# Output between the score halves, choice steps and one copy dealt anew, V read once a pass, projected rows' trips later

## The reference

```python
q = einsum('btc,hdc->bhtd', x, Wq); k = einsum('btc,hdc->bhtd', x, Wk)   # 16 heads of 64
w, sel = top_k(einsum('btc,hec->bthe', x, Ws), 2)                        # 2 of 8 experts per row and head
mix_v = einsum('bthk,bthke->bthe', sigmoid(w), one_hot(sel, 8))
v = einsum('bthe,bted->bhtd', mix_v, einsum('btc,edc->bted', x, Wv))
probs = softmax(einsum('bhid,bhjd->bhij', q * 64**-0.5, k), -1)
attn = einsum('bhij,bhjd->bihd', probs, v)
mask_o = one_hot(top_k(einsum('btc,hec->bthe', x, Wd), 2)[1], 8).sum(3)
res = einsum('bthe,bthd,efd->bthf', mask_o, attn, Wo).sum(2)
```

## Time and profile before

| | |
|---|---|
| median of 3 runs | 2452.25 us |
| the profiled execution | 2448.69 us |
| its span, first to last instruction | 2446.9 us |
| what lies around the span | 1.8 us |
| granted TensorE clock, mean | 0.993 |
| PE busy | 2341.4 us, 96% |
| ACT busy | 2079.9 us, 85% |
| DVE busy | 1964.1 us, 80% |
| POOL busy | 1138.2 us, 47% |

### The profile page before, as it was taken

The page is one execution under the profiler, slowest core; times in us unless marked ns, Lnnn a source line. Parts: engine busy times, 40 slices in busy tenths (PEclk is TensorE's granted clock), DMA queues, the critical chain, the costliest instruction groups (busy, mean ns, idle before and its releaser), DMA issues.

```text
span 2446.9 us, 120555 instructions
## 1 busy us (share of the span) xinstructions
PE 2341.4 (96%) x49920; PEld 2159.1 (88%) x49920; DVE 1964.1 (80%) x3498; ACT 2079.9 (85%) x6373; POOL 1138.2 (47%) x1126
## 2 busy tenths in 40 slices
PE   3999999999999999999999999999999999999997
PEld 3889989899999898989989999898899989999997
DVE  4887888878888887888888788788887888888874
ACT  2988888888888888888888888888888888889896
POOL 3354645445445455344444454454454553544441
PEclk8999999999999999999999999999999999999999
DMA  4555555555555655555555556555555555555563
GB/s 123 161 158 159 150 154 150 170 154 163 172 150 162 170 159 163 154 167 158 164 156 172 152 159 176 149 165 157 164 160 161 167 162 161 156 169 151 166 176 107
DMA packets 660701, 388.23 MB, mean 159 GB/s; under 512 B 232512, under 2 KB 585664, under 8 KB 660160
## 3 DMA queue, kind: packets, MB, share of 16 engines
q1 hardware_dynamic: 659728, 379.67, 54.0%
q10 hardware_dynamic: 432, 0.85, 0.1%
HBM read 191.64 MB, written 188.74 MB: 155 GB/s over the span
## 4 chain that ended last, share of the span: by engine, by line
PE 79%; DVE 9%; ACT 6%; issue 4%; POOL 1%; DMA 0%; SPq 0%; ACTq 0%; DVEq 0%; POOLq 0%
PE psT L466 17%; PE psS L421 14%; PE psT L483 6%; PE psS L509 6%; PE psT L434 6%; PE psT L485 5%; PE psT L484 5%; PE psT L509 5%; PE psT L478 5%; ACT PB L780 5%; PE psT L448 3%; DVE NMAX L660 1%; DVE QK L719 1%; DVE ST L742 1%; PE psT L515 1%
## 5 line engine op out<-in xcount | busy, mean ns | idle before, releaser
L780 ACT ACTIVATE PB<-psS,NMAX 128x256 f32<-128x256 f32 x2048 | 943.5, 488 | 76.7 <-DVE NMAX L660 73.6
L466 PE MATMUL psT<-V,PT 128*64 128x64 f32 x16384 | 548.2, 224 | 26.9 <-issue 25.9
L466 PEld LDWEIGHTS psT<-V,PT 128*64 128x64 f32 x16384 | 507.5, 138 | 57.5 <-issue 32.0
L719 DVE TENSOR_TENSOR QK<-psT,QK 128x512 fp32r<-128x512 f32 x512 | 340.6, 687 | 203.9 <-ACT QK L789 202.0
L421 PE MATMUL psS<-QK 64*128 64x256 f32 x6144 | 480.7, 291 | 0.0
L780 ACT ACTIVATION_READ_ACCUMULATOR PB<-psS,NMAX 128x1 f32 x2048 | 452.5, 221 | 0.0
L421 PEld LDWEIGHTS psS<-QK 64*128 64x128 f32 x6144 | 405.3, 187 | 31.7 <-issue 28.6
L660 DVE TENSOR_REDUCE NMAX<-psS 128x2 f32<-128x512 f32 x512 | 328.6, 683 | 84.1 <-PE psS L421 83.1
L789 ACT ACTIVATE QK<-psT 128x512 fp32r<-128x512 f32 x512 | 297.3, 624 | 91.2 <-PE psT L485 78.0
L888 POOL TENSOR_TENSOR BT<-MT,diagv 128x1024 f32<-128x1024 f32 x128 | 306.8, 2397 | 142.3 <-DMA MT<-MIXd 142.0
L869 ACT ACTIVATE PT<-psS 128x512 f32<-128x512 f32 x512 | 280.2, 604 | 52.1 <-PE psS L509 48.3
(11 more groups left out here) (119 smaller groups left out, 4578.2 us busy)
## 6 DMA issues: line engine op xcount, KB each, us to landing
Vd<-VM SPq DMA_DIRECT2D x512, 128.0 KB, 2.3
V<-Vd SPq DMA_DIRECT2D x512, 128.0 KB, 3.1
AOd<-AO SPq DMA_DIRECT2D x256, 256.0 KB, 2.7
AR<-AOd SPq DMA_DIRECT2D x256, 256.0 KB, 4.2
PJd<-PJ SPq DMA_DIRECT2D x64, 512.0 KB, 3.0
PR<-PJd SPq DMA_DIRECT2D x256, 128.0 KB, 2.6
MIXd<-MIX SPq DMA_DIRECT2D x64, 128.0 KB, 2.1
MT<-MIXd SPq DMA_DIRECT2D x64, 128.0 KB, 2.9
```

What stands on the lines that cost most here:

```text
L466: last = eng.matmul(M[64 * u:64 * u + 64, (t * NT + it) * DH:(t * NT + it + 1) * DH], PT[:, t, jt, cols], V[:, pm % 2, 4 * r + t, jt, :], ...
L719: eng.tensor_tensor(QK[:, 1, ab], bank("qk", m).rearrange("p (k t) -> p k t", k=2), QK[:, 0, ab].bitcast(F32), ALU.subtract).then_inc(free ...
L780: eng.activation(PB[:, ab, j, it, :], psS[:, ab, j, it, :], ACT.Exp, bias=NMAX[:, ab, j, it:it + 1], accum_out=SUM[:, p % 2, it, 4 * r + t ...
```

## The change

Six edits go together. The matrices, their shapes and the bank order stay as they are.

1. PE: in r = 1 `output(p-2)` stands between `scores(n, 0)` and `scores(n, 1)`.
2. DVE, r = 1: the statistics of pass p+3 and the additions of the output stand between the maxima of half 0 and of half 1, and `first(F1)` stands behind the AO copy.
3. DVE: `equal` of the first round moves ahead of the QK steps in r = 0; `equal` and `weigh` of the second round move from the end of r = 2 to right behind `largest`; the reciprocal of SG moves ahead of the AO copy in r = 3.
4. In r = 0 and r = 3 the copy of turned tile 3 goes from ACT to DVE, where it stands behind the QK steps and ahead of the pieces of g and of `weigh`.
5. SP: V is loaded whole in r = 0, in four parts of all 128 partitions, behind both stores of Vd.
6. SP: the store of PJ moves behind the store of AO in r = 2, and the load of PR in r = 3 waits until product(n-1) is full.

```diff
# SP
-            def load_values(q, half):
-                rows = slice(64 * half, 64 * half + 64)
+            def load_values(q):
                 eng.wait_ge(s_split, 4)
-                eng.wait_ge(s_vw[half], 16 * PARTS * (q + 1))
+                for half in range(2):
+                    eng.wait_ge(s_vw[half], 16 * PARTS * (q + 1))
...
                 if r == 0 and runs(p):
-                    load_values(p, 1)
+                    load_values(p)
...
-                if r == 3 and runs(p + 1):
-                    load_values(p + 1, 0)
+                if r == 3:
+                    wait_full(eng, "product", n - 1)
                 if r == 3 and runs(p + 2):
                     q = p + 2
                     eng.wait_ge(s_pjw, 16 * (q + 1))
# PE
                 if works(n):
                     scores(n, 0)
+                if r == 1 and runs(p - 2):
+                    output(p - 2)
+                if works(n):
                     scores(n, 1)
...
-                if r == 1 and runs(p - 2):
-                    output(p - 2)
# DVE
+                if r == 1 and runs(p + 3):
+                    wait_x(eng, p + 3)
+                    statistics(s_stat, 4 * (p + 3), 0, x_of(p + 3))
+                if r == 1 and runs(p - 2):
+                    for it in range(NT):
+                        xs = x_of(p - 2)[:, it, :]
+                        wait_full(eng, "output", p - 2, it)
+                        eng.scalar_tensor_tensor(xs, bank("output", p - 2, it)[:, 0:C], 0.5, xs, ALU.mult, ALU.add).then_inc(freed("output", p - 2, it))
+                if works(n):
                     eng.wait_ge(s_score, 2 * n + 2)
                     eng.tensor_reduce(NMAX[:, 1, :, :], psS[:, 1, :, :, :], AX_X, ALU.max, negate=True).then_inc(s_max)
...
                 if r == 2 and runs(q):
                     eng.wait_ge(s_pick, at + 6)
                     largest(1, GM[:, :, :])
+                    equal(1, GM[:, :, :], at + 7)
+                    weigh(at + 8)
...
+                if r == 1 and runs(q):
+                    if q >= 1:
+                        eng.wait_ge(s_share, SHARES * (q - 1) + 3)
+                    first(F1[:, :, :], at + 4)
                 if r == 0 and runs(q):
                     wait_freed(eng, "gates", q)
                     largest(0, GS[:, :, :])
+                    equal(0, GS[:, :, :], at + 1)
...
+                if works(n) and r in (0, 3):
+                    wait_turned(eng, n, 3)
+                    wait_full(eng, "product", n - 1)
+                    eng.tensor_copy(turned_rows(3), turned(n, 3).rearrange("p (k x) -> p k x", x=64)).then_inc(was_copied(n, 3))
                 if r == 0 and attends(p - 3):
# ACT
-                    for t in (2, 3, 0, 1):
+                    for t in (2, 0, 1) if r in (0, 3) else (2, 3, 0, 1):
```

More of the change, by code:

```diff
@@ L274, in wait_copied, with turned_rows @@
                 eng.wait_ge(s_copied[t - 2], n + 1)
+        def turned_rows(t):
+            ab, a = divmod(t, 2)
+            return PT[:, 2 * ab:2 * ab + 2].rearrange("p j k (i a x) -> p a (j k i) x", i=NT, a=2)[:, a]
         def wait_x(eng, p):
@@ L382, in sync_program @@
                     eng.dma_start(AOd[m // 4 % 2].rearrange("(p r x) -> p r x", p=P, r=4)[:, m % 4, :], AO[:, m % 2, :]).then_inc(s_aow[m % 2], 16)
+                if r == 2 and runs(p + 2):
+                    q = p + 2
+                    wait_freed(eng, "expert", q, 0)
+                    wait_freed(eng, "expert", q, 1)
+                    if q >= 2:
+                        eng.wait_ge(s_pr, 16 * PARTS * (q - 1))
+                    eng.dma_start(PJd[q % 2].rearrange("(p x) -> p x", p=P),
+                                  PJ[:, :, :, :].rearrange("p e n d -> p (e n d)")).then_inc(s_pjw, 16)
                 if r == 0 and runs(p - 1):
@@ L455, in product @@
                 if r == 0:
-                    eng.wait_ge(s_value[pm % 2], 32 * PARTS * (pm // 2 + 1))
+                    eng.wait_ge(s_value[pm % 2], 16 * PARTS * (pm // 2 + 1))
                 M = bank("product", m)
@@ L667, in vector_program @@
                     eng.reciprocal(RSUM[:, :], SUM[:, (p - 1) % 2].rearrange("p n h -> p (n h)")).then_inc(s_rsum)
[L668 to L672, removed]
                 if r == 2 and attends(p - 3):
@@ L675, in vector_program @@
                     statistics(s_bstat, 4 * nth[p - 3], 2, AA)
-                if r == 1 and runs(p + 3):
-                    wait_x(eng, p + 3)
-                    statistics(s_stat, 4 * (p + 3), 0, x_of(p + 3))
                 if r == 1 and runs(q):
                     highest(at + 3)
-                    if q >= 1:
-                        eng.wait_ge(s_share, SHARES * (q - 1) + 3)
-                    first(F1[:, :, :], at + 4)
                 if r == 2 and runs(q):
@@ L691, in vector_program @@
                     eng.tensor_scalar(SG[:, :, :], SG[:, :, :], 1.0, None, ALU.add).then_inc(s_pick)
+                    eng.wait_ge(s_pick, at + 12)
+                    eng.reciprocal(SG[:, :, :], SG[:, :, :]).then_inc(s_pick)
                 if works(n - 1):
@@ L719, in vector_program @@
                         eng.tensor_tensor(QK[:, 1, ab], bank("qk", m).rearrange("p (k t) -> p k t", k=2), QK[:, 0, ab].bitcast(F32), ALU.subtract).then_inc(freed("qk", m))
[L720 to L723, removed]
                 if r == 1 and runs(q):
@@ L748, in vector_program @@
                     weigh(at + 2)
-                if r == 2 and runs(q):
-                    weigh(at + 8)
                 if r == 3 and attends(p - 2):
@@ L864, in scalar_program @@
                 if works(n):
-                    for t in (2, 3, 0, 1):
-                        ab, a = divmod(t, 2)
+                    for t in (2, 0, 1) if r in (0, 3) else (2, 3, 0, 1):
                         wait_turned(eng, n, t)
                         wait_full(eng, "product", n - 1)
-                        eng.activation(PT[:, 2 * ab:2 * ab + 2].rearrange("p j k (i a x) -> p a (j k i) x", i=NT, a=2)[:, a],
-                                       turned(n, t).rearrange("p (k x) -> p k x", x=64), ACT.Copy).then_inc(was_copied(n, t))
+                        eng.activation(turned_rows(t), turned(n, t).rearrange("p (k x) -> p k x", x=64), ACT.Copy).then_inc(was_copied(n, t))
         @block.gpsimd
```

15 lines of the change are left out of this document (2 added, 13 removed).

## The result

The median of the kernel after is 2465.9 us (2457.65 to 2480.6, 9 runs), that of the kernel before, on the same chip, 2454.03 us (2450.22 to 2457.95, 9 runs). The ratio is 1.0056, with an interval of 1.0034 to 1.0078: slower by 0.56%, 12 us. The prediction said 2457, in 2434 to 2490, with "slower" the likeliest of the three by a little. The sign and the range held; of the sum behind them little did, as the rest of this document shows.

The account below looks back on a forecast made before the run. PE is busy 96% of the span, and in most quarters a DVE-ACT-DVE chain releases its last transposes. Terms +15 + 3 - 2 - 9 = +7, taken as +5: 2457 us by the median, range 2434 to 2490.

Parts of the forecast that it names:

- MT and BT 0.5 earlier ... then BT is always ahead of S, the 7 free passes are lost: Odd second quarters: S, ST and FW on DVE always queue behind POOL's BT; quarter 10.5 us, +15 us in all.
- with V's larger parts slower by 0.5, +28: Odd second quarters: upper bound of the +15 term, if V's larger parts land 0.5 us later.
- the longer chain: Odd second quarters: statistics and additions ahead of second maxima; first maxima to next scores 7.8 us, now 7.2.
- F1 behind MB: Rival, even second quarters: F1 waits 1.9 us for MB; +49, up to +95 with odd ones; chance 0.17 with GM.
- Passes 4 to 9, +3: Second quarters of passes 4 to 9: start slips by 1 us, quarter longer by about 0.5; +3 us.
- Even second quarters, 0: Even second quarters: the reordered chain stays hidden by PE, with F1 ahead of MB by 0.1 to 0.2 us; 0.
- The same race between GM and the second MB is worth +13: Even passes, inside a rival: GM caught behind the second MB, +13 us; chance 0.17 for F1 or GM.
- Last quarters -2: EQ and FW leave the way of r = 3's maxima: 0.15 us in 16 odd passes, even ones bound by PE; -2.
- stalls -9: PE's instruction-fetch stalls inside products, odd r = 3 and some even r = 2, shrink with quieter queues; -9, bounds 0 and -17.
- the stalls shrink and BT comes early: Rival: quiet queues shorten stalls by 14 us and BT starts 0.6 earlier than taken; 2438 us, chance 0.33 including BT.
- The rival with the least chance, 0.08: All edits hidden: tile copy does not wait, V's parts slower so FW passes BT; within 5 us, 2450; chance 0.08.

Follow-up runs that it names:

- values_whole_only: The kernel before with edit 5 alone (V read whole in the first quarter); 2431.1 us, ratio 0.9909.
- copy_only: The kernel before with edit 4 alone (copy of turned tile 3 on DVE in r = 0 and r = 3); 2466.43 us, ratio 1.0045.
- order_only: The kernel before with edits 1 and 2 alone (output between score halves, statistics and additions earlier, F1 behind AO); 2459.18 us, ratio 1.0016.
- copy_back: The kernel after without edit 4 (turned tile 3 copied by ACT again); 2434.62 us, ratio 0.9911.
- copy_behind_state: The kernel after with DVE's copy of tile 3 in r = 0 moved behind SV, S and ST; 2428.11 us, ratio 0.9894.
- copy_third_only: The kernel after with tile 3 copied by DVE in r = 3 alone and by ACT again in r = 0; 2433.64 us, ratio 0.9914.
- transfers_only: The kernel before with edits 5 and 6 alone (V whole in r = 0, PJ store later, PR behind the product); 2435.05 us, ratio 0.9919.
- behind_state_no6: The kernel after with the tile 3 copy behind S and ST in r = 0, and without edit 6; 2428.38 us, ratio 0.9908.
- mt_first: The kernel before with edit 5 alone, but with the load of MT issued ahead of V; 2491.61 us, ratio 1.0171.

## Why the prediction came out as it did

- **"MT and BT 0.5 earlier ... then BT is always ahead of S, the 7 free passes are lost"** is the step that failed. I took "the four parts of 256 KB at the pace of the four of 128 KB". They land in 4.0 us, not 3.1, and MT, issued behind them, in 5.0, not 2.9 (the pages of the two profiles). The issue of MT did move by 0.5, as forecast: in odd passes it stands at 5.12 of the first quarter, for 5.58 before (medians). The landing moved four times as far the other way. BT in odd passes starts at 1.78 behind the scores (median), before at 0.24. Blocked passes were freed, where I had the free ones lost: 20 at 9.52 and 5 at 11.7, and by chance the same mean, 9.95. The term was +15 and came out 0. (The count was off by one as well: before, FW, ST or S is blocked in 19 passes, and 6 are free, which makes the term +14.) The bound "with V's larger parts slower by 0.5, +28" named the slower parts and took the cost to grow with them; it does until BT starts behind ST and FW (between 1.24 and 1.41 of the quarter in the kernel after), and then it is gone. values_whole_only shows the mechanism by itself: 25 of 25 free, 9.44, which is 13 of the 22 us by which it is faster.
- **The working of the step was sound where its premise held.** With MT early, S waits behind BT in every odd pass (copy_only: BT at 0.12, maxima at 3.23, 10.46), and the longer chain costs 0.6 (order_only, 10.63 for 10.04). The two together with an early MT, the 10.5 of the sum, were not run without other edits. Left out was F1 behind MB in odd passes that are not blocked: 8 in order_only, 6 in copy_back, none in the kernel after, where MB starts 0.2 us or more behind F1.
- **Passes 4 to 9, +3.** Measured +7.1: 9.4 in their first quarters, some of it given back in the second. The cause that I gave, the slip of 1 at the second quarter's start, is not it. I costed the copy at 0.6 and 0.9 for DVE's instructions behind it, and did not ask which bank those free, though the bank order was at hand. copy_back and copy_behind_state both remove it.
- **Even second quarters, 0.** Nearly right in size, 8.86 with 8.77 before, +2 in all, but the race was another. The +2 is V's: it was to be issued 0.0 to 1.0 earlier, and in even passes it is issued at 3.57, for 2.45 (medians), and up to 5.5. "The same race between GM and the second MB is worth +13" stood in a rival; it came with the first MB, because POOL was late. Of the 0.61 us that even third quarters lost, it accounts for at most 0.36 (first maxima 1.11 to 1.47) and the gaps for at most 8.8 / 25 = 0.35; in part they overlap.
- **Last quarters -2 and stalls -9.** The last quarters gave -17. copy_third_only and copy_back, both near 9.09 and 9.0, show that the copy has no part in it. Edit 3 has, by elimination: the kernels without it (values_whole_only, transfers_only, order_only) have medians of 9.23 to 9.25 in even and in odd passes, those with it 9.08 to 9.10 and 8.95 to 8.96. So 0.15 a quarter comes in even passes too, which I had called bound by PE. Edit 3 was not run alone. Of the stalls the gaps' table shows -11 in last quarters and +9 in even third ones. Their sum stayed within 2.3 us, inside my bounds of 0 and -17 and far from the -9 I took. That they moved rather than shrank was not foreseen. Why the fetch comes later in even third quarters is not settled: in the traces PE goes on 1.2 to 1.6 us behind the end of a fetch, whatever the queues do.
- **Passes 0 to 3, +7,** were not in the prediction. Both the copy alone and the order alone bring them (copy_only 151.4, order_only 150.9), and without the copy 146.7 is left (copy_back). In the trace PE waits for issue ahead of the products in the second quarters of passes 0 and 1 for 3.05 and 2.28 us, before 1.37 and less than 0.4. These products want V, whose last part lands 0.1 us ahead of the end of either wait; why V comes later there stays open.
- **The sum.** +7 was worked out, of which +5 was taken, and +12 measured (17 between the profiled executions). The right sign came from a false term: in the real sum the transfers are worth some -20, the copy in the first quarter +31 to +38 in their company, the order +4, and edit 3 about -8 (the last quarters of values_whole_only against those of the kernel after). These make +7; the other 5 are not accounted for. That the copy costs 11 alone and 31 in their company lies mostly in third quarters, which won 8 us with it alone and lost 7 with it there; the gaps moved by -6 and by +8 us. The rival "the stalls shrink and BT comes early", 2438, had the time of the kernel without edit 4, but not its reason. BT was late, not early. The rival with the least chance, 0.08, had that half right: "V's parts are slower so that FW passes BT". Its other half, that the tile copy does not wait, was wrong (0.87 us in pass 31).

Best seen: the kernel after with the copy behind ST, 2428.11 us, and the kernel before with edit 5 alone, 2431.1. Their intervals overlap. What is open is a version of behind_state_no6 in which MT alone is held back in odd passes: by the table it could win up to the 20 us of odd second quarters without V being late. That is an estimate from the table; it was not tried.

## What to carry to other kernels

When an instruction that waits is put into an in-order engine, go through what stands behind it and ask of each which bank or buffer it frees: the same copy cost 38 us ahead of three small steps and nothing behind them. When a transfer is merged or moved, recompute the landing of the transfer behind it in the queue, and then every race that this landing decides; here a landing 1.7 us later won 13 us in odd second quarters (values_whole_only), about as much as the whole change lost. Do not exchange two loads in one queue before asking what each of them waits for.

## What the runs showed that was not expected

- A transfer's landing depends on what is ahead of it in its queue: MT, 128 KB, took 2.9 us behind half of V in 128 KB parts, 5.0 and 4.6 behind the whole of it (after, values_whole_only), 2.4 with nothing ahead (mt_first).
- A delay can pay. With MT 1.7 us later from issue to landing (4.6 for 2.9, values_whole_only) odd second quarters win 13 us, 0.5%, since short DVE steps pass ahead of a 2.4 us POOL instruction: ST takes 0.29 us when it starts first and 2.42 when it starts 0.1 behind BT.
- The gaps beside instruction fetches are not a fixed cost. With the same 400 fetches and the same matmuls in the same order, their sum over passes 10 to 59 was 18.2 us in values_whole_only, 32.0 in the kernel before and 44.9 in mt_first; the longest of the kernel after was 3.2 us.
